# Graph attention in two layers: two more source blocks transposed by DMA in layer 1, and the sums of a step closed one slot later

## What is computed

```python
q, k, v = (x @ Wq + bq), (x @ Wk + bk), (x @ Wv + bv)      # heads of 128 columns
alpha = einsum('ehc,ehc->eh', q[dst], k[src]) / sqrt(C)
p = exp(alpha - amax[dst])
denom = segment_sum(p, dst) + 1e-16
out = segment_sum(p[:, :, None] * v[src], dst) / denom[:, :, None]
out = concat_or_mean_over_heads(out) + x @ Ws + bs
```

## Time and profile before

| what | value |
|---|---|
| median of three runs | 1870.65 us (1866.98 to 1871.71) |
| the profiled execution | 1866.99 us, its span 1864.9 us |
| mean granted TensorE clock | 0.983 |
| TensorE busy | 1771.1 us, 95% of the span, 14,644 products |
| weight loads busy | 1330.1 us, 71% |
| VectorE busy | 1508.3 us, 81% |
| ScalarE busy | 1255.0 us, 67% |
| GpSimd busy | 1138.9 us, 61% |
| DMA, hardware queue of SyncE | 79.4% of 16 engines' time |

### The profile page before, as it was taken

The page is one execution under the profiler, slowest core; times in us unless marked ns, Lnnn a source line. Parts: engine busy times, 40 slices in busy tenths (PEclk is TensorE's granted clock), DMA queues, the critical chain, the costliest instruction groups (busy, mean ns, idle before and its releaser), DMA issues. The chain is left out here.

```text
span 1864.9 us, 44238 instructions
## 1 busy us (share of the span) xinstructions
PE 1771.1 (95%) x14644; PEld 1330.1 (71%) x14644; DVE 1508.3 (81%) x4506; ACT 1255.0 (67%) x2088; POOL 1138.9 (61%) x1432
## 2 busy tenths in 40 slices
PE   3789899999999999999999999989899999999997
PEld 2556567777777777777777777756677787777776
DVE  7999878888888888888888788724688888988886
ACT  4579777777777677777777777711466667766675
POOL 4200057777776777777677776723467676766765
PEclk9899999999999999999999999999999999999999
DMA  6779858877888888878778887690488999999996
GB/s 168 218 214 264 225 114 150 156 148 151 160 159 155 154 150 157 159 157 151 153 156 152 159 156 151 119 255 1 84 173 170 184 176 176 173 180 184 177 175 108
DMA packets 753647, 301.70 MB, mean 162 GB/s; under 512 B 655852, under 2 KB 734064, under 8 KB 750170
## 3 DMA queue, kind: packets, MB, share of 16 engines
q1 hardware_dynamic: 752252, 296.96, 79.4%
q0 software_dynamic: 640, 1.63, 0.3%
q10 hardware_dynamic: 528, 0.26, 0.1%
HBM read 93.62 MB, written 47.83 MB: 76 GB/s over the span
## 5 line engine op out<-in xcount | busy, mean ns | idle before, releaser
L1382 POOL TENSOR_TENSOR prob_parts_l<-prob_l,prob_parts_l 125x512 f16<-125x512 f32 x600 | 720.8, 1233 | 14.7 <-ACT prob_parts_l L1469 14.7
L1460 ACT ACTIVATE prob_l<-prob_l,neg_max_l 125x1024 f32<-125x1024 f32 (+1 forms) x450 | 521.5, 1161 | 4.8 <-DVE neg_max_l L1551 4.7
L1727 PE MATMUL score_l<-room,QT_l 128*128 128x512 f16 (+2 forms) x2100 | 512.9, 354 | 1.4 <-DVE scale_rows L1699 1.2
L1475 ACT CAST probT_l<-transposed_l 128x375 f16<-128x375 f32 x450 | 213.3, 474 | 430.3 <-PE transposed_l L1751 430.3
L1766 PE MATMUL output_l<-V,prob_flipped_l 128*128 128x256 f16 x2400 | 459.6, 272 | 4.9 <-DMA prob_flipped_l<-prob_parts_l 4.9
L1768 PE MATMUL output_l<-V,prob_flipped_l 128*128 128x128 f16 x2400 | 427.5, 219 | 0.0
L1543 DVE CUSTOM_DVE_ANT_0 prob_l<-score_l,mask_even 125x512 f32<-125x512 f32 (+2 forms) x546 | 334.0, 615 | 115.5 <-PE score_l L1727 115.0
L1543 DVE CUSTOM_DVE_ANT_0 prob_l<-score_l,mask_odd 125x512 f32<-125x512 f32 (+2 forms) x504 | 309.1, 615 | 107.7 <-PE score_l L1727 106.9
L1469 ACT CAST prob_parts_l<-prob_l 125x1024 f16<-125x1024 f32 x300 | 309.4, 1032 | 0.1
L1766 PEld LDWEIGHTS output_l<-V,prob_flipped_l 128*128 128x128 f16 x2400 | 233.7, 97 | 57.1 <-issue 7.1
L1766 PE MATMUL output_l<-V,probT_l 128*128 128x256 f16 x1350 | 271.4, 273 | 2.9 <-DVE probT_l L1556 1.6
(11 more groups left out here) (199 smaller groups left out, 2357.9 us busy)
## 6 DMA issues: line engine op xcount, KB each, us to landing
mask_scratch<-log SPq DMA_DIRECT2D x87, 420.0 KB
mask_even<-mask_scratch SPq DMA_DIRECT2D x25, 448.0 KB
mask_odd<-mask_scratch SPq DMA_DIRECT2D x24, 448.0 KB
mask_odd<-mask_scratch SPq DMA_DIRECT2D x12, 896.0 KB
mask_even<-mask_scratch SPq DMA_DIRECT2D x12, 896.0 KB
prob_flipped_l<-prob_parts_l SPq DMA_TRANSPOSE x600, 3.2
hT_scratch<-rowsT_l SPq DMA_DIRECT2D x24, 250.0 KB, 3.7
mask_odd<-mask_scratch SPq DMA_DIRECT2D x12, 471.2 KB
```

Of the source, the lines that this page charges most:

```text
L1382: pool.tensor_tensor(parts[0:TP, 1, a:b], prob[:, h % 2, a:b], parts[0:TP, 0, a:b], ALU.subtract).then_inc(s_flo, 1)
L1460: act.activation(e, e, ACT.Exp, bias=neg_max[:, h % 2:h % 2 + 1], accum_out=total[:, h % 2, c:c + 1]).then_inc(s_exp, 1)
L1475: act.copy(probT[:, q, 0, 0:n, 0:TP], flipped_in_psum(h, q, n)).then_inc(s_hi, 1)
L1727: last = pe.matmul(score_bank(h, p)[:, 0:b - a], QT[:, h % 2, i, :], KT[:, h, j, a:b], start=n == 0, stop=n == len(products) - 1)
```

## The change

In layer 1 five pieces (18 blocks) are transposed by DMA instead of four (16), and TensorE transposes the other two pieces, of four and three blocks. The pieces are cut anew for that: 4, 4, 4, 3, 3, 4, 3 blocks. The second half of the DMA pieces has three pieces and ten blocks. The exponentials follow the new parts: pieces 0 and 1, pieces 2 to 4, pieces 5 and 6. GpSimd's low parts are five instructions instead of four. TensorE's transposes are in slots 0 and 1, the values of its pieces in slots 2 and 3. The DMA pieces 0 and 1 are multiplied in slots 4 and 5, pieces 2 and 3 both in slot 6, and piece 4 in slot 0 of the next step; the sum is read in that step's slot 1. Layer 2 keeps its pieces, slots and sizes. To make room in SBUF, `v_back2` is now made at the start of layer 2's projections, by two VectorE instructions there, from the scale of the values, and the scale steps of layer 2 in layer 1 are eleven.

The diff, cut to its core:

```diff
-FB = 16
 CUTS = ((0, 512), (512, 1024), (1024, 1536), (1536, 2048), (2048, 2432), (2432, 2816), (2816, N))
-HALVES = ((0, 1), (2, 3))
-ND = 4
-NQ = len(CUTS) - ND
-EXP_PARTS = ((0, 1), (2, 3), (4, 5, 6))
+CUTS1 = ((0, 512), (512, 1024), (1024, 1536), (1536, 1920), (1920, 2304), (2304, 2816), (2816, N))
+DMA_PIECES = {1: 5, 2: 4}
+ND2 = DMA_PIECES[2]
...
-STEPS2 = 12
+STEPS2 = 11
...
                 link(dve.memset(V[:, NT - 1, :, :, :], 0.0))
+                v_back = L["v_back"]
+                link(dve.tensor_scalar(v_back[:, :].bitcast(I32), up[:, 2, :].bitcast(I32), -1, INVERSE, ALU.mult, ALU.add))
+                link(dve.tensor_scalar(v_back[:, :], v_back[:, :], 1.0 / P_UP, None, ALU.mult))
                 dve.wait_ge(s_colp, 1)
...
+    CUTS_OF = CUTS1 if layer == 1 else CUTS
+    ND = DMA_PIECES[layer]
+    NQ = NP - ND
+    HALVES = ((0, 1), tuple(range(2, ND)))
+    EXP_PARTS = HALVES + (tuple(range(ND, NP)),)
+    FB = CUTS_OF[ND][0] // C
+    FLIPPED_AT = {k: tuple(range(k - 4, ND - 1 if k == NP - 1 else k - 3)) for k in range(4, NP)}
+    QB = max(len(blocks_in(cut)) for cut in CUTS_OF[ND:])
...
-        probT = sb("probT", [C, NQ, 2, 3, C], F16)
+        probT = sb("probT", [C, NQ, 2, QB, C], F16)
...
                     if n == 8:
-                        power(back, v).then_inc(s_chain2, 1)
+                        power(v, v).then_inc(s_chain2, 1)
                     if n == 9:
-                        inverse(v, back).then_inc(s_chain2, 1)
+                        inverse(v, v).then_inc(s_chain2, 1)
                     if n == 10:
                         dve.tensor_scalar(v, v, V_UP, None, ALU.mult).then_inc(s_chain2, 1)
-                    if n == 11:
-                        dve.tensor_scalar(back, back, 1.0 / (V_UP * P_UP), None, ALU.mult).then_inc(s_chain2, 1)
...
                             if 2 <= k <= NQ + 1:
                                 values(s, h, k - 2)
-                            if k >= NP - ND + 1:
-                                flipped_values(s, h, k - (NP - ND + 1))
+                            if k >= 4:
+                                for p in FLIPPED_AT[k]:
+                                    flipped_values(s, h, p)
```

More of the change, by code:

```diff
@@ L181, in build @@
                 "V": sb2("V2", [C, NT, H2, 2, C], F16),
-                "v_back": second["v_back"],
+                "v_back": sb2("v_back2", [C, H2 * C]),
                 "Wq": second["W"][1],
@@ L841, in _ @@
                 dve.wait_ge(s_row, 16 * len(ROW_SPLIT))
-                for a, b in CUTS:
+                for a, b in CUTS1:
                     dve.scalar_tensor_tensor(first_mask[:, a:b], first_mask[:, a:b], STEEP, first_mask[:, a:b],
@@ L1068, in _ @@
                         sp.dma_start(mask[0][r0:r1, a:b], mask_dram[r0:r1, a:b]).then_inc(s_first[n], 16)
-                a, b = FIRST[0][0], CUTS[ND - 1][1]
+                a, b = FIRST[0][0], CUTS[ND2 - 1][1]
                 for r0, r1 in ROW_SPLIT:
@@ L1138, in _ @@
                             value_low(t - 1)
-                        if t >= CLEAR_FROM and t - CLEAR_FROM < NP + ND:
+                        if t >= CLEAR_FROM and t - CLEAR_FROM < NP + ND2:
                             row, piece = divmod(t - CLEAR_FROM, NP)
@@ L1148, in _ @@
                 value_low(NT - 1)
-                dve.wait_ge(s_cleared, NP + ND)
+                dve.wait_ge(s_cleared, NP + ND2)
             @block.tensor
@@ L1184, in attention @@
               mask=None, s_cleared=None, s_second=None):
-    v_back2 = second and second["v_back"]
     featT, KT, V, v_back, Wq, Ws, bq = (L[n] for n in ("featT", "KT", "V", "v_back", "Wq", "Ws", "bq"))
     W = H * C if layer == 1 else C
+    CUTS_OF = CUTS1 if layer == 1 else CUTS
[6 more added lines that the diff above has]
+    QB = max(len(blocks_in(cut)) for cut in CUTS_OF[ND:])
     with ExitStack() as ctx:
@@ L1251, in attention @@
         PART_PIECES = ((0, 1), (2, 3), (4, 5), (6,)) if layer == 1 else ((0, 1, 2, 3), (4, 5, 6))
-        MASK_PARTS = [(CUTS[pieces[0]][0], CUTS[pieces[-1]][1]) for pieces in PART_PIECES]
+        MASK_PARTS = [(CUTS_OF[pieces[0]][0], CUTS_OF[pieces[-1]][1]) for pieces in PART_PIECES]
         CLEAR_AT = ({(0, 2): 0, (0, 5): 1, (1, 2): 2, (1, 5): 3, (2, 1): 4, (2, 4): 5, (2, 6): 6} if layer == 1 else
@@ L1290, in half_cols @@
         def half_cols(half):
-            return CUTS[HALVES[half][0]][0], CUTS[HALVES[half][-1]][1]
+            return CUTS_OF[HALVES[half][0]][0], CUTS_OF[HALVES[half][-1]][1]
         with nc.Block() as block:
@@ L1376, in low_parts @@
                     for p in range(ND):
-                        a, b = CUTS[p]
+                        a, b = CUTS_OF[p]
                         half = half_of(p)
@@ L1458, in exponentials @@
                         act.wait_ge(s_max, s + 1)
[L1459 removed]
+                    e = prob[:, h % 2, CUTS_OF[EXP_PARTS[c][0]][0]:CUTS_OF[EXP_PARTS[c][-1]][1]]
                     act.activation(e, e, ACT.Exp, bias=neg_max[:, h % 2:h % 2 + 1],
@@ L1471, in high_part @@
                 def high_part(s, h, q):
-                    n = len(blocks_in(CUTS[ND + q]))
+                    n = len(blocks_in(CUTS_OF[ND + q]))
                     act.wait_ge(s_tp, NQ * s + q + 1)
@@ L1748, in transposes @@
                     pe.wait_ge(s_exp, EP * (s + 1))
-                    for i, b in enumerate(blocks_in(CUTS[ND + q])):
+                    for i, b in enumerate(blocks_in(CUTS_OF[ND + q])):
                         w = width_of(b)
@@ L1782, in flipped_values @@
                         pe.wait_ge(s_flip[half][n], 16 * (s + 1))
-                    for b in blocks_in(CUTS[p]):
+                    for b in blocks_in(CUTS_OF[p]):
                         hi, lo = (flipped[:, h % 2, n, b, :] for n in range(2))
```

2 lines of the change are left out of this document (removed).

## The result

The changed kernel takes 1902.09 us in the median (1901.49 to 1907.31) against 1870.18 us before: a ratio of 1.0187, with a 95% interval of 1.0174 to 1.0200. Its profiled execution has a span of 1900.4 us, 35.5 us more than before; the medians differ by 31.9, as the profiled execution of before was the fastest of its four.

The account below looks back on a forecast made before the run. TensorE was taken to bound layer 1, a ScalarE and VectorE chain 0.35 us behind. Steps +30 us, landings +4, less some of 6, gave about +31 on 1870.65: 1902 us, range 1866 to 1932.

Parts of the forecast that it names:

- The gain: Two TensorE transposes fewer in each of layer 1's 100 steps: 0.27 us a step, 27 us in all.
- The chain: Layer 1's first transposes, ScalarE copy and VectorE subtraction grow, so VectorE's read of the sum ends 0.36 us later.
- The steps of a tile: Layer 1: three steps at +0.21 us, the skip step at +0.56, together +1.19 a tile, +30 over 25 tiles.
- it is a plain loss: Everything of TensorE's is queued behind its 0.48 us wait for the first values, so the wait is lost.
- the stall: TensorE's wait before a step's first values: 0.48 us, 1.07 in the skip step; cost up to 0.06 smaller each.
- The DMA: Layer 1's ten-block half lands in 3.5 us, the low half's 1.5 us slack falls to nothing: 4 us.
- GpSimd's part: Low parts start 8.18 us after the step's first transpose, take 5.58; hidden by nothing to spare, else 2.5 us.
- One sign: In the new profile TensorE's busy time falls by some 20 us, yet its idle rises by more.
- The figures of the Trainium skill: By them two blocks more would add 5.2 us of DMA a step; the forecast rejected this.
- That TensorE stays the bound: Rival for layer 1: the time falls by 27 us to 1844; chance 0.13.
- The wash: Rival: the chain's links are half as long, stall near 0.27 us, time 1870 (1865 to 1876); chance 0.07.
- The landing rival: Rival: ten-block DMA half lands at 4.5 us or later, 50 us in all, 1950; half at 4.0; chance 0.12.

Follow-up runs that it names:

- run 10: Changed kernel with three blocks in the first TensorE group, late skip addition, new orders on ScalarE, TensorE, SyncE and GpSimd: 1848.01 us, ratio 0.9895.
- run 11: run 10 with the pieces of the kernel before, 16 blocks by DMA and nine on TensorE: 1861.70 us, ratio 0.9977.
- run 1: Changed kernel with the first TensorE group of three blocks and the second of four: 1889.05 us, ratio 1.0118.
- run 12: run 10 with the change's cut put back, four blocks in the first TensorE group: 1881.15 us, ratio 1.0063.
- Run 5: Changed kernel with the pieces and slots of before, the second half's DMA transfers carrying a ninth block of unread zeros: 1869.35 us, ratio 1.0009.
- run 2: Changed kernel with layer 1's skip addition moved on VectorE from slot 0 to the end of slot 1: 1888.36 us, ratio 1.0114.
- run 7: run 6 with ScalarE copying the first half right behind its exponential and TensorE's query ahead of the second group's values: 1877.69 us, ratio 1.0046.
- run 6: Changed kernel with the edits of run 1 and run 2 together: 1875.00 us, ratio 1.0045.

## Why the prediction was right, point by point

**The gain.** Two transposes of 0.137 us a step. It is real: runs 10 and 11 differ only in the pieces, that is in which way two blocks are transposed. I had 27 us for it; 15 came out, so this term was too large. The steps say where the rest is: in the median a tile's second, third and fourth step take 9.07, 9.06 and 9.07 us in run 10 and 9.29, 9.28 and 9.29 in run 11, 0.22 less each instead of 0.27. The first step gains nothing (11.07 and 11.05), and there the weight loads of the skip product wait 16.4 us in all for ScalarE's copy in run 10 and 10.6 in run 11.

**The chain.** Every link came within 0.04 us: the copy 0.58 (0.57 said), the subtraction 0.68, the read of the sum at T+2.65 (2.62), the values at T+2.77 (2.74), the skip step at T+3.37 (3.33), the row maximum at T+3.42 (3.39), the exponentials at T+3.46 (3.43). The load that comes 0.48 us late is what the rows show, and runs 1 and 12 show it as a cause, from both ends.

**The steps of a tile.** Forecast 11.12, 10.08 and 9.55 for the first three; measured 11.29, 10.08 and 9.42. The plain third step is 0.13 shorter than said. What the late load costs is read best between runs 12 and 10, which differ in the cut alone: the median plain step is 9.36 and 9.07 us, so a load that comes 0.48 us late costs 0.29. That TensorE makes the rest good behind the wait is my reading; the runs show only the difference. I had seen it in the skip step of before and allowed 0.06 for it; it is 0.13 to 0.19. So "it is a plain loss" was wrong, and the stall was the term that I sized worst.

The first step is longer for a wait that I had not followed: ScalarE copies the transposed rows behind the third exponential, which now ends later, and the skip product waits for that copy, 11.4 us in layer 1 on the weight loads where it was 5.6 in the kernel before.

The fourth step I had taken for a plain one. In the median it is nearly that, 9.49 us against 9.35 before, but in the mean it is 9.86 against 9.39: the late landings of the next paragraph fall there.

**The DMA.** I had 4 us for late landings. The idle time before DMA pieces went from 6 us to 22 us, 16 more, so that term was too small by some 12 us of idle time. Of the 22 us, 16.7 in 20 waits lie in the fourth steps of the tiles, where it was 1.2 in two waits before; why there, no run tests. The median landing is 3.4 us over all transfers of layer 1 and for the ten-block low halves too (I took 3.5), at worst 6.2. I had carried the median through and only guessed at the tail, with the slack gone to nothing.

```profile
DMA to landing us min/median/max: 3.0/3.4/6.2
```

GpSimd's part was right (low parts start at T+8.17 and take 5.58 us, said 8.18 and 5.58).

**The hit on the number** is in part luck. A stall and a gain that were both sized too large, landings sized too small and a longer first step came to 1.43 us a tile, 36 us in all, where I had 30 for the steps, 4 for the landings and some 3 taken off. I also added 3.7 us for the distance of the profiled execution of before from its median; from one profiled execution to the other the forecast was 31 us and the measured difference 35. One sign failed: TensorE's busy time fell by 8.0 us, not by some 20. That busy time is modelled, while the 0.137 us of a transpose is read from the starts of weight loads.

**The figures of the Trainium skill** ("VectorE: DVE Perf Modes", "The three transpose paths": TensorE 390 ns, DMA 1309 ns for a 128x128 block), taken as a price for each block, would have made the DMA the bound. Run 5 added a block to two transfers a step at no price, and run 10 is fastest with 18 blocks by DMA; the traces disagree with that, and the measurement decides. What the traces do show is that a DMA transpose lands 3.4 us after its issue in the median and 6.2 at worst, which matters as soon as its consumer has no slack.

**Rivals.** That TensorE stays the bound fell with the first row of the result. The wash fell with the time, though its stall of near 0.27 us is closer to the 0.29 of runs 12 and 10 than my 0.48: its links were wrong, as they came out at full length. The landing rival was wrong for most of the change's cost: runs 1 and 2 together take back 27 of the 32 us without touching the landings. It was right about what comes next: late landings hid the whole gain in run 7.

## What to carry to other kernels

Where one engine is busy 99.8% of the time, ask how far behind it the next chain is, and cost a change by both: here 0.27 us of saved work met a load that came 0.48 us late, and cost 0.29 by itself, because the first group of a chain had grown by one block. The tile's step with the skip addition and the late landings added to it. Make the first group of such a chain the small one, keep work that nobody waits for out of the queue ahead of the one instruction that releases the bound engine, and issue transfers in the order in which they are needed. When an edit that should pay does not, look for the next wait before giving it up: runs 6 and 7 stood at 1.0045 and 1.0046, and two edits of order later the same idea was at 0.9895.

## What I had not expected of the hardware

VectorE's clearing of a mask piece of 512 columns reads and writes SBUF alone, and yet its time varies from kernel to kernel with the same operands. Its mean is 1008 ns in the kernel before, 745 in the changed one and 708 in run 10. Single ones are longer still in the kernel before, as this one, where GpSimd had begun its subtractions 0.22 us earlier (at 616.18):

```profile
616.40 1.49 DVE L1529 SCALAR_TENSOR_TENSOR mask_even<-mask_even 125x512 f32<-125x512 f32 x1
```

In run 11, with the pieces of before and another order on GpSimd, the mean is 721 ns. The traces before, after and of runs 10, 11 and 12 say more. The 138 clearings in layer 1 during which no GpSimd instruction ran for more than 0.05 us all took 674 to 691 ns. Those with a GpSimd subtraction beside nearly all of them took 1377 ns in the median before (48 of them) and 1111 in run 12 (24), but 689 in the changed kernel (13). So the long ones occur only beside GpSimd, but not each one beside it is long, and what decides that no run tests.
